# A decoder of two layers on one core: the self attentions with 16 heads take their values as weights, in column groups

## The chip, the cores and the metric

The kernel runs on one core of one Trainium2 chip. The metric is the time of one execution on the device in microseconds. All stages run in one program, one after the other, each with its own order of work for the five engines.

## The reference, cut to what matters

Input `x` is 8 sequences of 112 tokens with 512 features. Six blocks follow one another: self attention, cross attention, a second self attention with a routed MLP (layer 0), then self attention with low-rank updates, a joint attention and a routed MLP (layer 1). The change touches the first and the fourth block:

```python
def _L0_attn_ref(x, Wq, Wk, Wv, Wo):          # HEADS = 16, Dh = 32, T = 112
    q = (x @ Wq).reshape(B, T, H, Dh)         # k, v alike
    scores = jnp.einsum('bthd,bshd->bhts', q, k)
    scores = scores * jnp.tril(jnp.ones((T, T)))
    attn = jax.nn.softmax(scores / T ** 0.5, axis=-1)
    out = jnp.einsum('bhts,bshd->bthd', attn, v).reshape(B, T, H * Dh)
    return out @ Wo
def _L1_attn_ref(x, Wq, bq, Bq, Aq, ...):     # HEADS = 16, HEAD_DIM = 32
    q = _split(lora_linear(x, Wq, bq, Bq, Aq))    # k, v alike
    attn = jax.nn.softmax(jnp.einsum('bhqd,bhkd->bhqk', q, k) * SCALE, axis=-1)
    out = jnp.einsum('bhqk,bhkd->bhqd', attn, v)  # transposed and reshaped to [B, L, 512]
    return lora_linear(out, Wo, bo, Bo, Ao)
x = x + _L0_attn_ref(_layernorm(x), ...)
x = x + _L1_attn_ref(_layernorm(x), ...)
```

The mask of the first is a product, not an addition of minus infinity. The second has no mask.

## The kernel before

Each stage is a `Segment`, made of parts. A part has a small program for each engine and yields at fixed places. The segment plays the parts against each other by a list of letters: each letter lets its part go on to its next yield, on every engine. Engines go in order; between them stand only semaphores. `self_attention_order` (L2969) writes the list for the two segments of the change, `self0` (L3407) and `self3` (L3480s). In both, `p` is `QkvPart` (the projections, which also split each weight into a high and a low part, the low part on GpSimd at L1353), `a` is `SelfAttentionPart` (L1466) and `o` is `OutNormPart` (L2037, the output projection and the norm).

The list first runs half of the projections, then one `a` and one `p` in turn; when the projections are used up, one `a` and one `o` in turn; what is left of `o` comes last.

`SelfAttentionPart`: an item is four heads of one sequence, in one tile of 112x448. A step takes two items and has two yields, so two `a` of the list; a sequence has four items and two steps, so there are 16 steps and two more to drain. In the first half of step s, TensorE transposes the probabilities of the items of step s-2 (L1578) and makes the scores of step s (L1589, two items in alternation, each in its own 32 rows of the array). VectorE multiplies by the mask (L1618, `self0` only) and takes maxima (L1622), GpSimd subtracts them (L1565; in `self3` VectorE does, L1625), ScalarE copies the transposed probabilities of step s-2 out of PSUM (L1652). In the second half ScalarE takes the exponentials of step s (L1656), TensorE multiplies the transposed probabilities, as weights, with the values (L1602, 128 columns, of which column 32 is a column of ones and so gives the sum), and VectorE takes the reciprocal of the sum (L1632) and evacuates four heads times it (L1640).

`OutNormPart`: for each sequence, TensorE transposes the attention's output (L2278), ScalarE and VectorE split it into high and low (L2127, L2179), TensorE multiplies with Wo (12 products, L2246 to L2250), VectorE adds to `x` and takes moments (L2190 on), GpSimd the power for the norm (L2118), VectorE normalises (L2215, or L2217 with rounding to L2222 in `self0`), and TensorE transposes the normed rows (L2260) for `hT_hi` (ScalarE, L2130) and `hT_lo` (VectorE, L2167). A sequence enters every fourth `o`. So each pair of `a` and `o` has four kinds: after the first half of odd steps stands the split of the output, after the first half of even steps the 12 products, the rounding and `hT`, and after the second halves normalisation (odd) or addition and moments (even).

What the part does with an attention depends on `attention.turned`; a part with `turned = True` is one whose output lies in PSUM with features on the partitions.

## Time and profile before

| | us |
|---|---|
| median of 3 runs | 2788.76 (2788.07 to 2790.92) |
| the profiled execution, own time | 2790.01 |
| its span, first to last instruction | 2788.1 |
| TensorE busy in the span | 2570.0 (92%) |
| VectorE busy | 1694.7 (61%) |
| ScalarE busy | 1132.2 (41%) |
| GpSimd busy | 896.6 (32%) |
| mean granted TensorE clock | 0.955 of full |
| steps with scores in the first attention | 202.7 to 300.4 |
| the same in the second attention | 1595.7 to 1702.5 |

Busy shares are means over stages with different limits. A row of the timeline gives start, length, engine, line, operation, output and inputs, the count, and in brackets how long the engine stood idle before it and who released it. Rows of an engine overlap a little where it pipelines, so the distance of two starts says more than the length. A float32 product stands as two records on TensorE, so eight products are "x16"; the float32 transposes of two items are eight instructions, and 8 of their records stand in the row.

### The profile page before, as it was taken

Reading aid. Unit: us, or ns where it says so; the run is one execution under the profiler, and the core shown is the slowest. Engines: PE = TensorE matmul, PEld = TensorE weight load, DVE = VectorE, ACT = ScalarE, POOL = GpSimd, SP = SyncE. Lnnn points to the kernel's source line nnn. Section 1 sums busy time; section 2 is a strip of 40 time slices with the busy share of each in tenths; the row PEclk is TensorE's granted clock in tenths of the full one; section 3 lists DMA queues with packets and bytes.
Section 4 is the critical chain, followed back from the end, with each engine's and each line's share of the span. In section 5 each row is a group of like instructions: output and inputs, shape, how many; then the busy total and the mean of one; then the engine's idle time right before and its main releaser. Section 6 shows DMA issues by size and latency. Waiting matters only on the chain. (4 is left out here: it accounts for less than half of the span.)

```text
span 2788.1 us, 48182 instructions
## 1 busy us (share of the span) xinstructions
PE 2570.0 (92%) x14667; PEld 2065.4 (74%) x14668; DVE 1694.7 (61%) x3341; ACT 1132.2 (41%) x2434; POOL 896.6 (32%) x919
## 2 busy tenths in 40 slices
PE   8999799979899989799997898998999999899998
PEld 7888677768688877678875777774665678788887
DVE  4537757769776657567675566864434325666664
ACT  2113255533343324445453133755555522444443
POOL 3213100014332225423223200753333322345555
PEclk9999999999899979899998898999999989999999
DMA  5553122125532045388774432444222031566664
GB/s 188 154 144 99 31 92 63 59 66 154 162 104 64 15 142 172 123 235 224 193 213 120 112 73 70 131 132 149 73 64 73 22 128 55 154 163 161 162 153 81
DMA packets 289277, 332.87 MB, mean 119 GB/s; under 512 B 147445, under 2 KB 202693, under 8 KB 287312
## 3 DMA queue, kind: packets, MB, share of 16 engines
q1 hardware_dynamic: 217904, 252.57, 29.1%
q0 software_dynamic: 20640, 51.74, 9.6%
q10 hardware_dynamic: 50560, 26.34, 3.3%
q8 instruction: 99, 1.62, 0.2%
q14 instruction: 74, 0.61, 0.1%
HBM read 233.86 MB, written 96.72 MB: 119 GB/s over the span
## 5 line engine op out<-in xcount | busy, mean ns | idle before, releaser
L898 PE MATMUL e_psum<-e_up_hi,hT_hi 128*128 x672 | 245.2, 365 | 21.5 <-DVE hT_lo L867 14.6
L900 PE MATMUL e_psum<-e_up_hi,hT_lo 128*128 x672 | 236.7, 352 | 0.0
L899 PE MATMUL e_psum<-e_up_lo,hT_hi 128*128 x672 | 236.4, 352 | 0.0
L1920 POOL TENSOR_TENSOR joint_a_p<-joint_a_p,joint_a_rinv 112x487 f32<-112x487 f32 x128 | 125.2, 999 | 195.9 <-DVE joint_a_rinv L1966 195.5
L1565 POOL TENSOR_TENSOR self_a_p<-self_a_p,self_a_mx 112x448 f32<-112x448 f32 x96 | 96.0, 1000 | 205.2 <-DVE self_a_mx L1622 205.2
L898 PEld LDWEIGHTS e_psum<-e_up_hi,hT_hi 128*128 128x128 f32 x672 | 127.5, 190 | 43.6 <-issue 32.3
L1971 DVE TENSOR_REDUCE joint_a_mx<-joint_psum 112x1 f32<-112x487 f32 x128 | 85.0, 664 | 121.5 <-PE joint_psum L1941 121.2
L794 ACT ACTIVATE e_gate<-e_psum 128x352 f32<-128x352 f32 (+1 forms) x86 | 44.4, 516 | 256.4 <-PE e_psum L900 252.1
L873 DVE TENSOR_TENSOR hT_lo<-e_psum,hT_hi 128x256 fp32r<-128x256 f32 (+2 forms) x138 | 55.7, 435 | 142.1 <-ACT hT_hi L812 139.0
L1656 ACT ACTIVATE self_a_p<-self_a_p 112x448 f32<-112x448 f32 x128 | 71.6, 575 | 164.8 <-POOL self_a_p L1565 113.8
L900 PEld LDWEIGHTS e_psum<-e_up_hi,hT_lo 128*128 128x128 f32 x672 | 127.5, 190 | 11.5
L899 PEld LDWEIGHTS e_psum<-e_up_lo,hT_hi 128*128 128x128 f32 x672 | 127.7, 190 | 9.7
L1209 POOL TENSOR_TENSOR p_p_z<-p_p_straight,p_p_crossed 128x512 f32<-128x512 f32 x70 | 98.4, 1406 | 112.1 <-DVE p_p_crossed L1191 112.1
L828 DVE TENSOR_TENSOR e_up_lo<-e_up_raw,e_up_hi 128x1024 f32 (+3 forms) x128 | 128.0, 1051 | 3.2 <-issue 3.0
L766 POOL DMA_INDIRECT out<-e_y,e_back x51 | 123.2, 2416 | 17.3 <-issue 17.3
L847 DVE SCALAR_TENSOR_TENSOR e_act_raw<-e_gate,e_rows,e_psum 128x352 f32<-128x352 f32 (+1 forms) x86 | 55.4, 645 | 118.3 <-ACT e_gate L794 115.9
L898 PE MATMUL e_psum<-e_dn_hi,hT_hi 128*128 (+1 forms) x285 | 121.3, 426 | 1.0 <-issue 0.3
L1941 PE MATMUL joint_psum<-x_first,x_q 128*112 128x487 f32 x256 | 117.8, 582 | 1.8 <-PEq L89 1.7
L752 POOL TENSOR_TENSOR e_held<-e_zeros 1x1 f32<-1x1 f32 x90 | 19.7, 218 | 308.2 <-DVE e_idx L862 308.2
L142 PE MATMUL p_psum<-p_p_w_hi,hT_hi 128*128 128x512 f32 x280 | 115.5, 412 | 1.9 <-DVE p_p_w_lo L1175 1.9
L1994 ACT ACTIVATE joint_a_p<-joint_psum,joint_a_neg 112x487 f32<-112x487 f32 x128 | 85.4, 667 | 75.8 <-DVE joint_a_neg L1973 72.5
L781 ACT ACTIVATE e_up_hi<-e_up_raw 128x1024 f32 (+3 forms) x128 | 107.8, 923 | 15.1 <-PEq L89 15.1
(561 smaller groups left out, 7484.6 us busy)
## 6 DMA issues: line engine op xcount, KB each, us to landing
e_up_raw<-in_L_ffn_w SPq DMA_DIRECT2D x64, 512.0 KB, 4.8
e_up_raw<-in_L_ffn_w SPq DMA_DIRECT2D x64, 352.0 KB
e_dn_raw<-in_L_ffn_w SPq DMA_DIRECT2D x16, 1024.0 KB, 14.2
q_all<-p_p_t_stage ACTq DMA_DIRECT2D x56, 256.0 KB
e_dn_raw<-in_L_ffn_w SPq DMA_DIRECT2D x16, 512.0 KB
x_q<-q_all SPq DMA_DIRECT2D x8, 896.0 KB
v_ctx<-front_c_v_stage SPq DMA_DIRECT2D x24, 250.0 KB
x_others<-k_ctx SPq DMA_DIRECT2D x8, 750.0 KB, 4.6
```

Source lines behind the costliest of these rows:

```text
L142: last = pe.matmul(out, a, b, start=(k == 0 and i == 0), stop=(k == n_k - 1 and i == len(pairs) - 1))
L766: pool.indirect_dma_start(out=acc, out_offset=bass.IndirectOffsetOnAxis(ap=back[:, v, :], axis=0), in_=y[:, v, :], in_offset=None, compute ...
L781: act.activation(up_hi[:, bass.ds(slot * KC + k, 1), :], up_raw[:, k:k + 1, :], ACT.Copy).then_inc(up_hi_ready, 1)
L828: dve.tensor_tensor(up_lo[:, bass.ds(slot * KC + k, 1), :], up_raw[:, k:k + 1, :], up_hi[:, bass.ds(slot * KC + k, 1), :].bitcast(F32), AL ...
L898: pe.matmul(out, lhs[0], rhs[0], start=k == 0, stop=False)
L899: pe.matmul(out, lhs[0], rhs[1], start=False, stop=False)
L900: return pe.matmul(out, lhs[1], rhs[0], start=False, stop=k == n_k - 1)
L1209: both = pool.tensor_tensor(z[:, r, :], straight[:, r, :], crossed[:, r, :], ALU.add)
L1565: pool.tensor_tensor(p[:, i % RING, :, :], p[:, i % RING, :, :], mx[:, i % RING, :].unsqueeze(2).to_broadcast([T, group, T]), ALU.subtract ...
L1920: pool.tensor_tensor(p[:, r, :], p[:, r, :], rinv[:, r:r + 1].to_broadcast([T, S]), ALU.mult).then_inc(p_ready, 1)
L1941: pe.matmul(ps[0:T, s_banks[i % N_S], 0:S], q[:, b % 2, h, :], k[:, b % 2, h // group, :], start=True, stop=True).then_inc(s_done, 1)
L1994: act.activation(p[:, r, :], ps[0:T, s_banks[i % N_S], 0:S], ACT.Exp, bias=neg[:, r, :], scale=scale, accum_out=rsum[:, r:r + 1]).then_inc ...
```

## The change

`HeadSelfAttentionPart` takes the place of `SelfAttentionPart` in `self0` and `self3`. It has the same items, steps and lags, and is played by the same list. What differs:

- Values are the weights (112x32 of one head) and the transposed probabilities the moving operand. Four heads go to four column groups of the array, 32 columns each, and so to four groups of PSUM partitions: the output of a sequence lies with features on the partitions, 128x448. All 16 products of a sequence are made at once, in the second half of every second step.
- There is no column of ones. VectorE sums the exponentials of step s-1 in the second half of step s and takes one reciprocal for both items. GpSimd multiplies the exponentials by it. TensorE's transposes (lag 2 as before) wait for that product instead of for the exponentials.
- `OutNormPart` reads the output from PSUM (`turned`): its transposes of the output and its wait for VectorE's evacuation are gone, and so is the evacuation itself.
- The transposed probabilities have a ring of six instead of two.

```diff
+class HeadSelfAttentionPart:
...
+        dh, group, W, n_items, n_steps = 32, 4, 2, 4, 2
+        RING, PT, LT, LE = 6, 6, 2, 2
+        self.n_items, self.steps, self.lead, self.turned = 2 * n_steps, 2 + 2 * (B * n_steps + LE), 2 * LE, True
+        q = g.sb(f"{name}_q", [128, 2, 4, T])
+        k = g.sb(f"{name}_k", [128, 2, 4, T])
+        v = g.sb(f"{name}_v", [T, 2, D])
+        p = g.sb(f"{name}_p", [T, RING, group, T])
+        pt = g.sb(f"{name}_pt", [T, PT, group, T])
...
+        self.ot_done, self.o_used = pv_done, None
...
+        def rows_of(i):
+            r = i % n_items
+            return slice(r * dh, (r + 1) * dh)
...
+        def ot_view(i):
+            return ps[:, o_banks[i % N_O], 0:group * T].rearrange("p (c t) -> p c t", c=group)
+        self.ot_view = ot_view
...
+        def gpsimd(pool):
+            yield
+            yield
+            for step in range(n_all + LE):
+                for i in pair(step) if mask else []:
+                    pool.wait_ge(mx_ready, i + 1)
+                    pool.tensor_tensor(p[:, i % RING, :, :], p[:, i % RING, :, :], mx[:, i % RING, :].unsqueeze(2).to_broadcast([T, group, T]),
+                                       ALU.subtract).then_inc(less_ready, 1)
+                yield
+                for i in pair(step, 1):
+                    pool.wait_ge(rinv_ready, i // W + 1)
+                    pool.tensor_tensor(p[:, i % RING, :, :], p[:, i % RING, :, :], rinv[:, i % RING, :].unsqueeze(2).to_broadcast([T, group, T]),
+                                       ALU.mult).then_inc(p_ready, 1)
+                yield
+
+        def tensor(pe):
+            yield
+            yield
+            for step in range(n_all + LE):
+                for i in pair(step, LT):
+                    pe.wait_ge(p_ready, i + 1)
+                    reuse(pe, pt_ready, i - N_T + 1)
+                    for j in range(group):
+                        last = pe.transpose(ps[0:T, t_banks[i % N_T], j * T:(j + 1) * T], p[:, i % RING, j, :], core.ident[0:T, 0:T])
+                    last.then_inc(t_done, 1)
+                both = pair(step)
+                if both:
+                    b = step // n_steps
+                    if step % n_steps == 0:
+                        pe.wait_ge(qk_in[b % 2], 32 * (b // 2 + 1))
+                    reuse(pe, mask_done if mask else less_ready, both[-1] - N_S + 1)
+                    for j in range(group):
+                        for i in both:
+                            last = pe.matmul(ps[0:T, s_banks[i % N_S], j * T:(j + 1) * T], q[rows_of(i), b % 2, j, :],
+                                             k[rows_of(i), b % 2, j, :], start=True, stop=True)
+                            if j == group - 1:
+                                last.then_inc(s_done, 1)
+                yield
+                at = step - LT
+                if at >= 0 and at % n_steps == n_steps - 1:
+                    b = at // n_steps
+                    pe.wait_ge(v_in[b % 2], 16 * (b // 2 + 1))
+                    pe.wait_ge(pt_ready, (b + 1) * n_items)
+                    reuse(pe, self.o_used, b - N_O + 1)
+                    for j in range(group):
+                        for i in range(b * n_items, (b + 1) * n_items):
+                            h = j * group + i % n_items
+                            last = pe.matmul(ps[rows_of(i), o_banks[b % N_O], j * T:(j + 1) * T], v[:, b % 2, h * dh:(h + 1) * dh],
+                                             pt[:, i % PT, j, :], start=True, stop=True)
+                    last.then_inc(pv_done, 1)
+                yield
...
+            for step in range(n_all + LE):
+                for i in pair(step):
...
+                yield
+                before = pair(step, 1)
+                for i in before:
+                    dve.wait_ge(exp_done, i + 1)
+                    dve.tensor_reduce(rsum[:, i % RING, :], p[:, i % RING, :, :], AX.X, ALU.add).then_inc(sum_ready, 1)
+                if before:
+                    at = before[0] % RING
+                    dve.wait_ge(sum_ready, before[-1] + 1)
+                    dve.reciprocal(rinv[:, at:at + W, :], rsum[:, at:at + W, :]).then_inc(rinv_ready, 1)
+                yield
...
+                for i in pair(step, LT):
+                    act.wait_ge(t_done, i + 1)
+                    reuse(act, pv_done, (i - PT) // n_items + 1)
...
@@ head_qkv, self0, self3 @@
-            return 32, p, lambda b: q32[b], lambda b: k32[b], lambda b: v_self[b, 0, 0:T, :], 16
+            return p, lambda b: q32[b], lambda b: k32[b], lambda b: v_self[b, 0, 0:T, :]
-                    a = SelfAttentionPart(g, "a", *head_qkv(p), float(T) ** -0.5, (2, 3), (4, 5), (6, 7), "tril", ALU.mult)
+                    a = HeadSelfAttentionPart(g, "a", *head_qkv(p), float(T) ** -0.5, (2, 3), (4, 5), (6, 7), "tril")
-                a = SelfAttentionPart(g, "a", *head_qkv(p), 32.0 ** -0.5, (2, 3), (4, 5), (6, 7))
+                a = HeadSelfAttentionPart(g, "a", *head_qkv(p), 32.0 ** -0.5, (2, 3), (4, 5), (6, 7))
```

On TensorE, in the steady part of the first attention, before: transposes of one item, the scores of the next step, then the output part's transposes.

```order
L1578 MATMUL self_psum<-ident,self_a_p 112x112 [waits self0_a_pt_ready,self0_a_exp_done]
L1578 MATMUL self_psum<-ident,self_a_p 112x112 x3
L1589 MATMUL self_psum<-self_a_k,self_a_q 112x112 [waits self0_a_mask_done]
L1589 MATMUL self_psum<-self_a_k,self_a_q 112x112 x7
L2278 MATMUL self_psum<-ident,self_a_o 128x112 [waits self0_o_lo_ready,self0_a_o_evac]
L2278 MATMUL self_psum<-ident,self_a_o 128x112 x3
```

Now:

```order
L1750 MATMUL self_psum<-ident,self_a_p 112x112 [waits self0_a_pt_ready,self0_a_p_ready]
L1750 MATMUL self_psum<-ident,self_a_p 112x112 x3
L1760 MATMUL self_psum<-self_a_k,self_a_q 112x112 [waits self0_a_mask_done]
L1760 MATMUL self_psum<-self_a_k,self_a_q 112x112 x7
L1774 MATMUL self_psum<-self_a_pt,self_a_v 32x112 [waits self0_o_lo_ready,self0_a_pt_ready,self0_a_v_in0]
L1774 MATMUL self_psum<-self_a_pt,self_a_v 32x112 x15
L1750 MATMUL self_psum<-ident,self_a_p 112x112 [waits self0_a_pt_ready,self0_a_p_ready]
```

The transposes wait for `p_ready` (GpSimd's product) instead of `exp_done`; the scores still stand behind them. Of the output part's transposes nothing is left, and the 16 value products are one group.

On VectorE, at the end of the first half of a step and through its second half, before:

```order
L1618 TENSOR_TENSOR self_a_p<-self_psum,self_a_mask 112x448 [waits self0_a_t_done,self0_a_s_done]
L1622 TENSOR_REDUCE self_a_mx<-self_a_p 112x4 [waits self0_a_mask_done]
L1402 COPY self_p_stage<-self_psum 112x512 [waits self0_p_stored3,self0_p_mm_done]
L2179 TENSOR_TENSOR self_o_oT_lo<-self_psum,self_o_oT_hi 128x448 [waits self0_o_hi_ready]
L1632 RECIPROCAL self_a_rinv<-self_psum 112x4 [waits self0_a_pv_done]
L1640 TENSOR_TENSOR self_a_o<-self_psum,self_a_rinv 112x4x32 [waits self0_a_rinv_ready]
L1632 RECIPROCAL self_a_rinv<-self_psum 112x4 [waits self0_a_pv_done]
L1640 TENSOR_TENSOR self_a_o<-self_psum,self_a_rinv 112x4x32 [waits self0_a_rinv_ready]
```

Now (`L1790` is the mask, `L1794` the maxima, `L2345` the low part of the output):

```order
L1790 TENSOR_TENSOR self_a_p<-self_psum,self_a_mask 112x448 [waits self0_a_t_done,self0_a_s_done]
L1794 TENSOR_REDUCE self_a_mx<-self_a_p 112x4 [waits self0_a_mask_done]
L1402 COPY self_p_stage<-self_psum 112x512 [waits self0_p_stored3,self0_p_mm_done]
L2345 TENSOR_TENSOR self_o_oT_lo<-self_psum,self_o_oT_hi 128x448 [waits self0_o_hi_ready]
L1803 TENSOR_REDUCE self_a_rsum<-self_a_p 112x4 [waits self0_a_exp_done] x2
L1807 RECIPROCAL self_a_rinv<-self_a_rsum 112x8 [waits self0_a_sum_ready]
L1790 TENSOR_TENSOR self_a_p<-self_psum,self_a_mask 112x448 [waits self0_a_t_done,self0_a_s_done]
```

Two evacuations with two reciprocals make place for two sums and one reciprocal, in the same position behind the mask and the maxima.

On GpSimd, from the start of `self0`, before:

```order
L2110 MEMSET self_o_expo 112x1
L1353 TENSOR_TENSOR x_others<-self_p_w_raw,x_others 128x512 [waits self0_p_hi_ready] x4
L1565 TENSOR_TENSOR self_a_p<-self_a_p,self_a_mx 112x448 [waits self0_a_mx_ready] x8
L1353 TENSOR_TENSOR x_first_lo<-self_p_w_raw,x_first_hi 128x512 [waits self0_p_hi_ready] x4
L1565 TENSOR_TENSOR self_a_p<-self_a_p,self_a_mx 112x448 [waits self0_a_mx_ready] x6
L2872 MEMSET x_others 128x6x96 [waits self0_p_mm_done]
L2118 TENSOR_TENSOR self_o_rstd<-self_o_var_eps,self_o_expo 112x1 [waits self0_o_var_ready,self0_o_expo_set]
```

Now (`L1733` subtracts the maxima, `L1738` multiplies by the reciprocals):

```order
L1353 TENSOR_TENSOR x_others<-self_p_w_raw,x_others 128x512 [waits self0_p_hi_ready] x4
L1733 TENSOR_TENSOR self_a_p<-self_a_p,self_a_mx 112x448 [waits self0_a_mx_ready] x4
L1738 TENSOR_TENSOR self_a_p<-self_a_p,self_a_rinv 112x448 [waits self0_a_rinv_ready] x2
L1733 TENSOR_TENSOR self_a_p<-self_a_p,self_a_mx 112x448 [waits self0_a_mx_ready] x2
L1738 TENSOR_TENSOR self_a_p<-self_a_p,self_a_rinv 112x448 [waits self0_a_rinv_ready] x2
L1733 TENSOR_TENSOR self_a_p<-self_a_p,self_a_mx 112x448 [waits self0_a_mx_ready] x2
L1353 TENSOR_TENSOR x_first_lo<-self_p_w_raw,x_first_hi 128x512 [waits self0_p_hi_ready] x4
L1738 TENSOR_TENSOR self_a_p<-self_a_p,self_a_rinv 112x448 [waits self0_a_rinv_ready] x2
L1733 TENSOR_TENSOR self_a_p<-self_a_p,self_a_mx 112x448 [waits self0_a_mx_ready] x2
```

The products stand between the subtractions, in pairs. Those of the third step's pair stand behind the split of Wo (`x_first_lo`, four instructions).

## Rows read from the trace of the kernel before

**Rows 1.** Windows, a steady stretch: busy us (instructions) of each engine, then PEclk, DMA share, GB/s.
```profile
260.00:280.00 20.00, 18.80 (x166) 16.48 (x164) 18.28 (x45) 7.54 (x15) 6.83 (x8) 0.91 0.29 66
```

**Rows 2.** Timeline, TensorE, score products and last value products, first attention: start, duration.
```profile
208.76 1.04 PE L1589 MATMUL self_psum<-self_a_k,self_a_q 32*112 32x112 f32 x16
245.24 1.04 PE L1589 MATMUL self_psum<-self_a_k,self_a_q 32*112 32x112 f32 x16
300.37 1.04 PE L1589 MATMUL self_psum<-self_a_k,self_a_q 32*112 32x112 f32 x16
313.90 1.97 PE L1602 MATMUL self_psum<-self_a_v,self_a_pt 112*112 112x128 f32 x16 [0.35 <-ACT self_a_pt L1652]
```

**Rows 3.** Timeline, TensorE, score products of the second attention.
```profile
1601.66 1.04 PE L1589 MATMUL self_psum<-self_a_k,self_a_q 32*112 32x112 f32 x16
1648.84 1.04 PE L1589 MATMUL self_psum<-self_a_k,self_a_q 32*112 32x112 f32 x16
1702.47 1.04 PE L1589 MATMUL self_psum<-self_a_k,self_a_q 32*112 32x112 f32 x16
```

**Rows 4.** Timeline, TensorE, one batch of the first attention.
```profile
276.02 1.04 PE L1589 MATMUL self_psum<-self_a_k,self_a_q 32*112 32x112 f32 x16
277.43 1.91 PE L1602 MATMUL self_psum<-self_a_v,self_a_pt 112*112 112x128 f32 x16
279.19 0.93 PE L1578 MATMUL self_psum<-ident,self_a_p 112*112 112x112 f32 x8
280.70 1.04 PE L1589 MATMUL self_psum<-self_a_k,self_a_q 32*112 32x112 f32 x16 [0.59 <-DVE self_a_p L1618]
284.67 0.55 PE L2260 MATMUL self_psum<-ident,self_p_w_raw 112*128 112x112 f32 x4
```

**Rows 5.** Timeline, VectorE, projection phase (first row) and the same batch.
```profile
212.47 0.62 DVE L1398 COPY self_p_stage<-self_psum 128x448 f32<-128x448 f32 x1 [0.17 <-PE self_psum L1453]
...
274.19 0.62 DVE L2167 TENSOR_TENSOR hT_lo<-self_psum,hT_hi 128x448 fp32r<-128x448 f32 x1 [0.76 <-ACT hT_hi L2130]
276.11 0.17 DVE L1632 RECIPROCAL self_a_rinv<-self_psum 112x4 f32<-112x4 f32 x1
278.75 0.62 DVE L1618 TENSOR_TENSOR self_a_p<-self_psum,self_a_mask 112x448 f32<-112x448 f32 x1
279.41 0.62 DVE L1622 TENSOR_REDUCE self_a_mx<-self_a_p 112x4 f32<-112x448 f32 x1
281.13 0.61 DVE L2179 TENSOR_TENSOR self_o_oT_lo<-self_psum,self_o_oT_hi 128x448 fp32r<-128x448 f32 x1
281.66 0.17 DVE L1632 RECIPROCAL self_a_rinv<-self_psum 112x4 f32<-112x4 f32 x1
282.49 0.54 DVE L2217 TENSOR_SCALAR self_p_w_raw<-x_tok,self_o_mv,self_o_rstd 112x512 f32<-112x512 f32 x1
```

**Rows 6.** Timeline, GpSimd and ScalarE, first attention.
```profile
226.22 5.01 POOL L1353 TENSOR_TENSOR x_first_lo<-self_p_w_raw,x_first_hi 128x512 fp32r<-128x512 f32 x4
231.19 1.83 POOL L1565 TENSOR_TENSOR self_a_p<-self_a_p,self_a_mx 112x448 f32<-112x448 f32 x2
...
273.61 0.54 ACT L2130 ACTIVATE hT_hi<-self_psum 128x448 fp32r<-128x448 f32 x1 [3.13 <-PE self_psum L2260]
```

**Rows 7.** Timeline, TensorE, an idle stretch, the window behind it, and scores at the lower clock.
```profile
267.50 1.04 PE L1589 MATMUL self_psum<-self_a_k,self_a_q 32*112 32x112 f32 x16 [1.14 <-DVE self_a_p L1618]
...
268.60:272.00 3.40, 3.40 (x8) 2.47 (x9) 3.16 (x10) 1.43 (x3) 0.42 (x1) 0.52 0.43 114
...
752.84 1.84 PE L1589 MATMUL self_psum<-x_first_hi,x_wp_hi 64*112 64x112 f32 x16 [0.23 <-DVE self_a_p L1618]
```

**Rows 8.** One VectorE line (min/median/max ns), its slow one, and GpSimd beside it.
```profile
L2221 DVE TENSOR_SCALAR self_p_w_raw<-self_p_w_raw x8: 426/427/1039, 261.5 to 339.2; 112x512 f32<-112x512 f32 x8
261.50 1.04 DVE L2221 TENSOR_SCALAR self_p_w_raw<-self_p_w_raw 112x512 f32<-112x512 f32 x1
261.14 1.10 POOL L1565 TENSOR_TENSOR self_a_p<-self_a_p,self_a_mx 112x448 f32<-112x448 f32 x1 [0.25 <-DVE self_a_mx L1622]
```

69 lines of the change are left out of this document (added).

## The prediction

> **What bounds the kernel now.** I read in this order: the busy time by stage, the spacing of the score products on TensorE, then each engine through one batch.
>
> In a step of an attention two items (four heads each) pass. TensorE transposes the probabilities of two steps ago (T), makes this step's scores (S) and lies one step ahead. VectorE masks and takes maxima (phase A1), then evacuates values (phase A2). One phase of the output part stands after each; "even" and "odd" steps differ in which. In the steady stretch VectorE is busy 18.28 of 20 us and TensorE 18.80 [rows 1]: both are near full, and neither waits long. S waits only for the mask of the step before (idle 0.59 us) [rows 4]. The ten steps of the first attention that carry no projections take 300.37 - 245.24 = 55.13 us for nine intervals [rows 2]; in the second 1702.47 - 1648.84 = 53.63 [rows 3]. The five intervals before them take 36.48 and 47.18 us; projections fill TensorE there.
>
> **The change, engine by engine.** VectorE loses two evacuations per step, 282.49 - 281.66 = 0.83 us [rows 5]. It gains two row sums of 112x448; the nearest row is the maximum of the same shape, 0.62 us, and four such operations of A1 go at 281.13 - 278.75 = 2.38, so two cost 1.19. One reciprocal with its gap adds 0.22 (0.17 and 0.05). That is +0.58 us per step.
>
> TensorE loses four transposes of the output per batch, 277.43 - 276.02 - 1.04 = 0.37 us, and its 16 value products, 2 x (279.19 - 277.43) = 3.52 us, become 16 of 32 output rows [rows 4]. The trace has no column groups. The nearest row is S, which alternates two row groups: 8 products in 1.04 us, 0.13 each; a value product takes 0.22. So 16 cost 2.1 us, with bounds 0.9 (four abreast) and 3.5 (no overlap). I take 2.1; it doesn't enter the sum, as TensorE gets idle time.
>
> GpSimd gains 32 multiplications per attention. The subtraction of the same shape is the nearest row: two in 1.83 us [rows 6].
>
> The price is in a wait. T of step s-1 used to wait for exponentials, long ready. It now waits for the multiplication, which waits for the reciprocal, which stands in A2 of step s behind A1 of step s. And S of step s+1 stands behind that T on TensorE, while A1 of step s+1 waits for S. So every step becomes one closed loop: S, A1, output phase, sums, reciprocal, multiplication, T, S. What VectorE does after the reciprocal (1.4 to 1.8 us of output work) lies beside it and hides nothing of it.
>
> Loop without output work: S 1.04 [rows 4], hop 0.03, A1 2.38, sums 1.19, reciprocal 0.22 [rows 5], hop 0.05, two multiplications 1.83 [rows 6], hop 0.05, second half of T 0.43 (0.93 for eight records, rows 4). Sum 7.22 us. From A2 to the next S it is 3.77.
>
> - Odd steps add oT_lo, 281.66 - 281.13 = 0.53 [rows 5]: 7.75.
> - Even steps of the first attention: step 6 adds nothing (7.22); step 8 adds the rounding, 276.11 - 274.19 - 0.53 = 1.39 (8.61). From step 10 hT_lo waits for ScalarE, which waits for transposes behind the 12 output products: 284.67 - 280.70 = 3.97 after S begins [rows 4], 0.58 for the transposes, 0.57 for ScalarE (0.54 long, rows 6), hT_lo 0.53, rounding 1.39, then 3.77: 10.81.
> - In the second attention there is no rounding: 7.22 for steps 6 and 8, 9.42 from step 10.
>
> First: 7.22 + 8.61 + 3 x 10.81 + 4 x 7.75 = 79.3, against 55.1: +24.1. Second: 2 x 7.22 + 3 x 9.42 + 4 x 7.75 = 73.7 against 53.6: +20.1.
>
> Steps 1 to 5, first attention. A projection's evacuation comes between A1 and A2: it starts 212.47 - 208.76 = 3.71 after S, lasts 0.54, then 3.77: 8.0 us. Steps 1 and 2 take that. In step 3 the multiplications stand behind Wo's split, 5.01 us [rows 6], and that behind this step's subtractions: A1 ends 3.45 after S, subtraction 0.98, split 5.01, multiplication 1.83, T 0.48: 11.75. Steps 4 and 5 with the wider value groups about 8.4 and 8.9. Sum 45.1 against 36.5: +8.6. Second attention: its five steps already take 9.4 us on the mean, more than the 8.0 to 8.9 of the loop, so only its shorter steps can grow, and no subtraction stands before the split. I estimate +3.5, between 0 and the first one's 8.6. Bounds of both together: 0 (hidden under projections) and 17.
>
> Tail: from S of step 15 to the last value products 313.90 - 300.37 = 13.5 us now. Then: 7.75, output products and transposes 2.93 + 0.58, ScalarE to rounding 2.49, 3.77, one copy 0.5: 18.0, less 0.4 for the output's transposes: +4.1. The same 4 for the second. Bounds 0 and 6 each.
>
> Sum at full clock: 24.1 + 20.1 + 8.6 + 3.5 + 8.1 = 64.4 us.
>
> **Clock.** TensorE would work some 8 to 9 us of the 15 to 18.6 of a batch, in bursts with 3 to 5 us of idle between. TensorE had idled 1.14 us before 267.50, and the granted clock was 0.52, the 1.2 GHz level, from 268.6 to 272.0 [rows 7]; so it will fall often. At that level S takes 1.84 us [rows 7] against 1.04, +0.8 on the loop, and the half T of 0.43 about +0.4 if it doubles: 21.6 us for 18 steps. Eight of twelve output products took 3.40 us there against 2.0 at the other level's 0.25 (3.0 over 12, rows 4): +1.4 to 1.6 in six steps, 9.6. All low costs 31, none 0. I take half, 15.
>
> 64.4 + 15 = 79.4. The profiled execution took 2790.0 us (span 2788.1 and 1.9 around it), so 2869.4; the median of before lies 1.2 lower: **2868 us**.
>
> **Port.** A scaling of 112x512 on VectorE took 1.04 us instead of 0.43 with a subtraction of 1.10 instead of 0.93 beside it on GpSimd [rows 8]: the two engines can hold each other up. The multiplication starts 0.05 after the reciprocal, just when h (0.54) starts on VectorE in the odd steps. I take nothing for it and keep up to 8 us for the range (0.5 in five odd steps of the first, 1.1 in the second, which adds a bias too).
>
> The Trainium skill, "SBUF — State Buffer", section "SBUF: two separate sides", says that the pair of ports shared by VectorE and GpSimd is locked for a whole instruction, by VectorE operations in a two-port mode or with two SBUF inputs, against a GpSimd operation that reads SBUF. The slow row agrees. By it the 8 us would fall due, and the time would be 2876.
>
> **Rivals.**
>
> 1. *VectorE's queue alone decides.* Normalisation hides behind output work, and the time grows by 0.58 x 36 steps at most: 21 us, likelier 10, as the early steps have slack: 2800. For it: VectorE is the fuller of the engines late in a batch. Against: the order of waits leaves no room. Chance 0.06.
> 2. *The loop closes only in the steady steps*, at full clock; projections and tail hide the rest: 44.2 us, 2833. Chance 0.12.
> 3. *The clock stays low and the port costs its 8*: 64 + 31 + 8 = 103, 2892. Chance 0.13.
> 4. *Faster: TensorE bounds and the wait is hidden.* Its stream has 18.80 of 20 us busy. Each batch frees 3.52 - 2.1 + 0.37 = 1.8 us, 29 for 16 batches: 2760. It decides if the multiplications end before TensorE comes to T, that is if TensorE has some 3.5 us of other work between S and T more than VectorE has. Only steps with two projection groups come near. Chance 0.04. The Trainium skill, "TensorEngine Tiling (Array Packing)", section "Theoretical Speedup", gives up to 4x for a dimension of 32; with it the value products would cost 0.9 us and this case would end at 2741. The trace shows 0.13 against 0.22 us for two groups, and no four.
> 5. *The change does nothing that can be measured*: sums, products and waits balance. Chance 0.03.
>
> **Numbers.** The forecast has 0.62: loop closed throughout, clock between the levels, 2850 to 2885. With rivals 2 and 3 the range is 2828 to 2893; 0.13 lies below with rivals 1, 4, 5, the rest is error of the terms. A measurement of this kernel tells about 0.2% from none. Slower by more than that: 0.62 + 0.12 + 0.13 + 0.06 = 0.93; same 0.03; faster 0.04.
>
> **What would show it.** In the profile after, T's first product waits for the multiplication in nearly every step, VectorE's mask waits for S some 1.5 to 2 us per step, and VectorE's busy share in both attentions falls although it has more work. S to S is near 7.7 in odd and 9.5 to 11 in even steps. In the projection phase of the first attention one interval is near 12 us, behind Wo's split. The granted clock is well under 1.00 there. Outside both attentions nothing moves. If T waits for nothing, or S to S stays near 6 us, the central step is wrong; if intervals are right at full clock, only the clock term is.

## The result, and the profile after

The changed kernel takes **2910.9 us** (2908.0 to 2914.65, 4 runs) against 2788.64 of the kernel before in the same job: ratio 1.0436, 95% interval 1.0423 to 1.0449. The forecast was 2868 with a range of 2828 to 2893: the direction and the mechanism hold, the size does not. The profiled execution has a span of 2912.9 us against 2788.1 and a mean granted clock of 0.923 against 0.955. These two spans differ by 124.8 us, the medians by 122.3, so 2.5 us of what follows is the spread of single executions.

The steady steps of both attentions first, as windows of the kernel after (columns as in [rows 1]), from the scores of step 6 to those of step 15:
```profile
258.12:353.97 95.85, 62.26 (x417) 46.69 (x416) 56.48 (x118) 22.69 (x43) 37.22 (x42) 0.62 0.16 46
1723.19:1813.98 90.79, 58.74 (x417) 43.60 (x417) 54.68 (x102) 24.86 (x47) 22.40 (x23) 0.67 0.14 38
```
They answer to the 55.13 and 53.63 us of [rows 2, 3]. There TensorE and VectorE were both near full. Now TensorE is busy 62 of 96 us and VectorE 56: no engine is full, and the clock is 0.62. That is the look of a closed loop.

Timeline of the kernel after, first attention, the loop of one odd step (start, length, and in brackets idle and releaser):
```profile
284.93 1.77 PE L1760 MATMUL self_psum<-self_a_k,self_a_q 32*112 32x112 f32 x16
286.63 1.72 PE L1774 MATMUL self_psum<-self_a_pt,self_a_v 112*32 112x112 f32 x32
286.72 0.62 DVE L1790 TENSOR_TENSOR self_a_p<-self_psum,self_a_mask 112x448 f32<-112x448 f32 x1 [2.59 <-PE self_psum L1760]
289.11 0.61 DVE L2345 TENSOR_TENSOR self_o_oT_lo<-self_psum,self_o_oT_hi 128x448 fp32r<-128x448 f32 x1
289.63 1.14 DVE L1803 TENSOR_REDUCE self_a_rsum<-self_a_p 112x4 f32<-112x448 f32 x2
290.81 0.20 DVE L1807 RECIPROCAL self_a_rinv<-self_a_rsum 112x8 f32<-112x8 f32 x1
291.09 2.02 POOL L1738 TENSOR_TENSOR self_a_p<-self_a_p,self_a_rinv 112x448 f32<-112x448 f32 x2 [0.89 <-DVE self_a_rinv L1807]
292.27 1.89 PE L1750 MATMUL self_psum<-ident,self_a_p 112*112 112x112 f32 x8 [3.92 <-POOL self_a_p L1738]
294.09 1.84 PE L1760 MATMUL self_psum<-self_a_k,self_a_q 32*112 32x112 f32 x16
296.01 0.62 DVE L1790 TENSOR_TENSOR self_a_p<-self_psum,self_a_mask 112x448 f32<-112x448 f32 x1 [3.48 <-PE self_psum L1760]
300.02 0.55 PE L2426 MATMUL self_psum<-ident,self_p_w_raw 112*128 112x112 f32 x4
```
Read it as a ring: scores to mask 1.79 us (1.07 predicted), phase A1 2.39 (2.38), oT_lo 0.52 (0.53), sums 1.18 (1.19), reciprocal 0.28 (0.27), products and last transposes 3.00 (2.31). Sum 9.16 against 7.75. Every VectorE step is right to 0.02 us; both excesses are TensorE at its lower level (scores 1.77 to 1.84 where [rows 4] had 1.04; eight transposes 1.89 for 0.93), but for 0.2 on GpSimd, whose pair takes 2.02 with VectorE's h beside it. In the even step behind it, the transposes that follow the output products start 300.02 - 294.09 = 5.93 us after the scores, where [rows 4] had 3.97.

The wait itself, over both attentions (one line of the kernel after, the transposes, and what its engine idled for):
```profile
L1750 PE MATMUL self_psum<-ident,self_a_p x256: 258/392/438, 214.8 to 1833.9; 112*112 112x112 f32 x128
its engine sat idle before it (us, times) until:
  POOL self_a_p L1738: 102.6, 46
```

Where the 124.8 us of span went, by starts of the score products and of the next stage (the tail is the time from the scores of step 15 to the next stage):

| part | predicted | measured |
|---|---|---|
| steps 6 to 14, first / second | 24.1 / 20.1 | 40.7 / 37.2 |
| steps 1 to 5, first / second | 8.6 / 3.5 | 13.5 / 4.9 |
| tail, first / second | 4.1 / 4.0 | 7.1 / 10.9 |
| clock, all parts | 15 | in the rows above |
| outside both attentions | 0 | 10.6 (not due to the change, see below) |
| start of the first scores, both together | 0 | 0.0 |

The rows for step 1 and the tail (answering to [rows 2]), and those of steps 3 to 5:
```profile
208.12 1.04 PE L1760 MATMUL self_psum<-self_a_k,self_a_q 32*112 32x112 f32 x16
...
224.72 1.84 PE L1760 MATMUL self_psum<-self_a_k,self_a_q 32*112 32x112 f32 x16
237.38 1.84 PE L1760 MATMUL self_psum<-self_a_k,self_a_q 32*112 32x112 f32 x16
248.93 1.04 PE L1760 MATMUL self_psum<-self_a_k,self_a_q 32*112 32x112 f32 x16
258.12 1.84 PE L1760 MATMUL self_psum<-self_a_k,self_a_q 32*112 32x112 f32 x16
...
353.97 1.84 PE L1760 MATMUL self_psum<-self_a_k,self_a_q 32*112 32x112 f32 x16
375.79 1.72 PE L1774 MATMUL self_psum<-self_a_pt,self_a_v 112*32 112x112 f32 x32 [0.67 <-issue]
```
Step 3 takes 12.66 us (11.75 predicted, behind Wo's split). Step 4 takes 11.55 where 8.4 was predicted; VectorE's next row says why, beside TensorE's products of the same time:
```profile
244.27 0.63 PE L1453 MATMUL self_psum<-x_others,hT_hi 128*112 128x512 f32 x2
244.47 0.69 DVE L1402 COPY self_p_stage<-self_psum 112x512 f32<-112x512 f32 x1 [2.76 <-PE self_psum L1453]
```
The projection's evacuation, ahead of the row sums, starts 244.47 - 237.38 = 7.09 us after the scores instead of 3.71 [rows 2, 5]. TensorE is not idle in between: it makes the scores in 1.84 us and then twelve products of the projection, 0.43 us each from start to start at its lower level and 0.23 where the clock is up again (244.27 on).

### The profile page after: what moved, and what is told of

It is laid out like the page before. It is cut to its first block and busy times, and to the rows that moved or that the text cites. A ratio compares the mean times of both kernels' runs of the same rounds, so it can differ in the third digit from the quotient of the medians.

```text
span 2912.9 us, 48005 instructions
## 1 busy us (share of the span) xinstructions
PE 2592.0 (89%) x14603; PEld 2057.0 (71%) x14604; DVE 1712.4 (59%) x3309; ACT 1134.8 (39%) x2434; POOL 955.9 (33%) x981
## 5 line engine op out<-in xcount | busy, mean ns | idle before, releaser
L2137 DVE TENSOR_REDUCE joint_a_mx<-joint_psum 112x1 f32<-112x487 f32 x128 | 85.0, 664 | 122.6 <-PE joint_psum L2107 122.3
L1750 PE MATMUL self_psum<-ident,self_a_p 112*112 112x112 f32 x256 | 51.5, 348 | 102.8 <-POOL self_a_p L1738 102.6
L1738 POOL TENSOR_TENSOR self_a_p<-self_a_p,self_a_rinv 112x448 f32<-112x448 f32 x64 | 63.2, 1008 | 182.7 <-DVE self_a_rinv L1807 182.7
L1750 PEld LDWEIGHTS self_psum<-ident,self_a_p 112*112 112x112 f32 x256 | 33.7, 173 | 121.5 <-POOL self_a_p L1738 121.4
L766 POOL DMA_INDIRECT out<-e_y,e_back x51 | 113.8, 2231 | 16.7 <-issue 16.7
```

The lines of the kernel that those rows point to most:

```text
L766: pool.indirect_dma_start(out=acc, out_offset=bass.IndirectOffsetOnAxis(ap=back[:, v, :], axis=0), in_=y[:, v, :], in_offset=None, compute ...
L1750: last = pe.transpose(ps[0:T, t_banks[i % N_T], j * T:(j + 1) * T], p[:, i % RING, j, :], core.ident[0:T, 0:T])
L2137: dve.tensor_reduce(mx[:, r, :], ps[0:T, s_banks[i % N_S], 0:S], AX.X, ALU.max).then_inc(mx_ready, 1)
```

## Experiments

Theory L: the closed loop through the wait is the cause. Rival W: the added operations themselves are. Theory C: a large part of the loop's length is TensorE's clock, which is low in a loop that leaves TensorE idle. Ratios are to the kernel before in the same job, with the 95% interval in square brackets. "Stages" are the first and second attention against before, which has 0 and 0; the changed kernel has +60.7 and +53.6.

**Scores first.** TensorE makes a step's scores before the transposes that wait.
```
             for step in range(n_all + LE):
-                for i in pair(step, LT): ... transposes
                 both = pair(step)          # scores
                 ...
+                for i in pair(step, LT): ... transposes
```


> In each step TensorE makes the scores of step s before the transposes of step s-2; nothing else is changed. Theory L (the closed loop of scores, masks, sums, product, transposes): scores no longer stand behind the product, so the loop opens; VectorE's queue decides, 0.58 us per step more than before. In the profile scores to scores go back to about 6.5 to 7 us, the granted clock in both attentions is above 0.95, and the time is 2805 us (2790 to 2820). Rival W (the added work itself, the shared port and the changed value products cost the time, wherever the scores stand): the time stays within 15 us of 2911.

2850.95 us, 1.0227 [1.0208, 1.0247]: stages +21.8 and +29.8. Half of the loss is gone by order alone, less than L expected (2805, bounds 2790 to 2820). The trace has another loop in its place, over two steps: steps 12 and 13 of the first attention take 17.4 us together, where the changed kernel takes 23.1 and the kernel before 12.7. Timeline of this kernel, TensorE and VectorE:
```profile
295.44 1.04 PE L1754 MATMUL self_psum<-self_a_k,self_a_q 32*112 32x112 f32 x16
296.12 0.62 DVE L2333 TENSOR_TENSOR hT_lo<-self_psum,hT_hi 128x448 fp32r<-128x448 f32 x1 [4.06 <-ACT hT_hi L2296]
298.04 1.14 DVE L1803 TENSOR_REDUCE self_a_rsum<-self_a_p 112x4 f32<-112x448 f32 x2
300.49 1.89 PE L1762 MATMUL self_psum<-ident,self_a_p 112*112 112x112 f32 x8 [4.00 <-POOL self_a_p L1738]
```
The scores wait no more, but the output products and their turn stand behind the waiting transposes; VectorE waits 4.06 us for their result, and the row sums stand behind that.

**Product left out, and done twice.** The first leaves the normalisation out (its output is not normalised); the second lets GpSimd make each product once more, into a spare tile.
```
-  for i in pair(step, 1): pool.tensor_tensor(p.., rinv.., mult).then_inc(p_ready, 1)
-  pe.wait_ge(p_ready, i + 1)
+  pe.wait_ge(exp_done, i + 1)
```


> GpSimd's multiplication is left out (the output is not normalised) and the transposes wait for the exponentials; the sums and reciprocals stay, and so do the new value products. Theory L: as with scores first, about 2800 us (2785 to 2815), a little less since GpSimd holds no port. Rival W in the form that sums or value products cost the time: above 2850. The distance to scores first tells what the product costs by its work alone: under 10 us.

> Each multiplication on GpSimd is made twice, the first into a tile that nobody reads. Theory L: every step's loop gets 2 x 0.93 us longer, in 16 to 17 steps of each attention: 33 x 1.86 = +61 us against 2911, so 2972 (2960 to 2985). A theory in which the product is mostly hidden and low clock comes from elsewhere gives under +15.

Left out (two executions): 2818.4 us, 1.0102, stages +2.6 and -0.2, although row sums and reciprocals are still there. What it takes over before is not in the attentions: the stretch with the experts between them took 34.8 us more, and its weight loads of the first product count 288 instead of 264. I take it that other values route tokens otherwise; no run tests that. Twice (two executions): 2996.42, 1.074: +85.5 us for 32 x 1.86 = 60 us of work, above L's bounds (2960 to 2985). In the steady steps the loop charges the price and a hand-over: an odd step of the first attention takes 11.3 us for 9.24. Most of the rest is in steps 1 to 5, which grow by 35 us in both attentions for 19 of work; from step 3 on their scores now take 1.84 us, and the mean granted clock of the whole is 0.906. Both speak for L, against W.

**Product on VectorE.** The same product behind the reciprocal, on VectorE (1.16 us the pair).
```
                     dve.reciprocal(...).then_inc(rinv_ready, 1)
+                    dve.wait_ge(rinv_ready, before[0] // W + 1)
+                for i in before:
+                    dve.tensor_tensor(p.., p.., rinv.., ALU.mult).then_inc(p_ready, 1)
```


> The product of probabilities and reciprocals stands on VectorE, right behind the reciprocal, instead of GpSimd. Theory L: the loop has 2 x 0.62 = 1.24 us in place of 1.83 and two hops of 0.05, so each of 36 steps is 0.69 us shorter, 25 us in all, 2886 us, though VectorE has 40 us more to do. Rival W (VectorE's work is what costs): 1.24 x 32 = 40 us more, 2950.

2883.85 us, 1.033 [1.0314, 1.0346]: 27 less than the change (29 less if each is taken against before in its own job), 25 expected, with some 37 us (32 x 1.16) more for VectorE to do. The shorter ring wins over the fuller engine: W falls.

**Three steps late.** The transposes take the probabilities of three steps ago, so that the product is a step old.
```
-        RING, PT, LT, LE = 6, 6, 2, 2
+        RING, PT, LT, LE = 6, 6, 3, 3
```


> The transposes take the probabilities of three steps ago instead of two; three value groups of buffers more, one more step of drain in each attention, no operation added or left out. Theory L (closed loop: TensorE's transposes wait for a product made in the same step): the product that they need is now a step old, nothing waits for it, the scores start as soon as the mask is done. Both attention stages return to before plus VectorE's 0.58 us a step where VectorE is full, plus one more step of drain (5 to 8 us each): 2788 + 8 + 13 = about 2809 us, bounds 2795 to 2825. The granted clock in the steady steps rises with it. Rival W (the added work itself costs, wherever it stands): within 15 us of 2911.

2799.13 us, 1.0028 [1.0017, 1.004]; stages -1.4 and +8.0. One step more of distance takes back 114 of 122 us with every added operation in place (8 are left against before in the same job), as L expected (2809, bounds 2795 to 2825). It does not make the change a gain. The transposes' line in this kernel:
```profile
L1750 PE MATMUL self_psum<-ident,self_a_p x256: 257/259/437, 218.7 to 1724.0; 112*112 112x112 f32 x128
its engine sat idle before it (us, times) until:
  POOL self_a_p L1738: 15.0, 13
```
15.0 us of waiting instead of 102.6, and a median of 259 ns instead of 392. The granted clock over the steady steps is 0.78 and 0.74, above the 0.62 and 0.67 of the changed kernel, but well below the 0.97 that both attentions had before: with the wait went part of the lower clock, not most of it.

**Filled idle time**, twice: products that nothing reads, between a step's scores and the next transposes; 24 from step 6, then 20 in the first attention from step 3 and 14 in the second from step 6.
```
+                if both and step >= 6:
+                    pe.wait_ge(pt_ready, W * (step - LT) + W)
+                    for _ in range(24): pe.matmul(<64 spare columns>, ident, ident[.., 0:64])
```


> From step 6 on, TensorE makes 24 small products without use in the second half of each step (112x64 of the identity, into a free part of a transposes' bank), about 2.6 us at the full clock, in the time in which it waits for GpSimd. Theory C (low clock is what the forecast mis-sized: some 25 us in each attention over the sum at full clock): granted clock above 0.95 in the steady steps, odd steps near 7.9 and even ones near 11 us, and the time falls by 25 to 40 us, to 2871 to 2886. Rival P (the shared port and longer hand-overs are the missing time, and the low clock is idle time that costs nothing): the time stays within 8 us of 2911 or rises.

> Adds idle-time products (20 in the first attention from step 3, 14 in the second from step 6) on TensorE between a step's scores and the next transposes, into a part of a bank that nothing reads; fewer than the 24 tried before, so that they end before the product that the transposes wait for. Theory C (of the 124 us, a large part is TensorE's clock at its lower level, because the loop leaves it idle): granted clock 0.9 or more from step 6 on in both attentions, odd steps 8.0 and even ones 9.4 to 10.8 as in the first filled run, now in both attentions: 25 to 40 us less than 2911, so 2871 to 2886. Rival P (the loop's length is set by VectorE and GpSimd alone, TensorE's pace doesn't matter): within 8 us of 2894, the first filled run, or above it.

24 (two executions): 2894.25, 1.0374; 14 and 20: 2921.6, 1.046 [1.0441, 1.048], 11 us worse than no filling. As totals both miss C's numbers, and the second is on its rival's side. The 24 take 4.8 us at the full clock, not the 2.6 expected. The filling delays the loop itself while the clock is low (20 products took 4.06 us before the score products of step 13 and 7.73 before the next; step 6 with 24 took 11.9 us for 8.2), and in the second run it did not hold the clock. What they do settle is the loop at full clock. Windows of the first filled kernel, steps 7 to 14 of both attentions:
```profile
271.63:345.54 73.91, 70.96 (x765) 63.40 (x765) 51.11 (x107) 20.54 (x40) 32.50 (x36) 1.00 0.12 33
1722.18:1797.58 75.40, 71.70 (x766) 64.38 (x765) 49.11 (x91) 22.35 (x44) 19.95 (x20) 0.98 0.17 46
```
The same steps of the changed kernel:
```profile
266.35:353.97 87.62, 54.33 (x381) 40.88 (x380) 51.60 (x110) 20.48 (x39) 33.05 (x37) 0.63 0.11 32
1731.31:1813.98 82.67, 51.03 (x381) 38.05 (x381) 49.63 (x93) 22.65 (x43) 20.58 (x21) 0.67 0.15 41
```
Transposes and scores of the first filled kernel around one odd step:
```profile
307.87 1.04 PE L1760 MATMUL self_psum<-self_a_k,self_a_q 32*112 32x112 f32 x16
314.51 0.58 PE L1750 MATMUL self_psum<-ident,self_a_p 112*112 112x112 f32 x4
315.39 0.59 PE L1750 MATMUL self_psum<-ident,self_a_p 112*112 112x112 f32 x4 [0.30 <-POOL self_a_p L1738]
315.91 1.04 PE L1760 MATMUL self_psum<-self_a_k,self_a_q 32*112 32x112 f32 x16
```
In the first attention, at clock 1.00, an odd step takes 8.04 us (7.75 predicted) and each even one from step 10 takes 10.79 (10.81 predicted); in the changed kernel they take 9.2 from step 9 on and 13.3 to 14.2. Steps 7 to 14 take 73.9 us here and 87.6 there: 13.7 us are clock. In the second attention they take 75.4 and 82.7: at least 7.3 us are clock, for here the filling itself outlasts GpSimd's product in some even steps (in step 8 the product ends at 1737.40 and the transposes start at 1739.19). The first attention's tail is 60.1 us at clock 0.72 in the changed kernel and 56.1 at 0.88 here: another 4.0.

**Sums on TensorE.** Can the feature-major form pay? Ones as weights give the sums in column groups, VectorE divides per sequence behind the value products; no row sums, no product on the ring.
```
+  for j, i: pe.matmul(ps[rows_of(i), o_banks[1], ..], ones[:, :], pt[:, i % PT, j, :])
+  dve.reciprocal(o[:, :, :], total); dve.tensor_tensor(o[:, :, :], out, o[:, :, :], ALU.mult)
```


> The value products keep their column groups and the output its feature-major form, but nothing is normalised before the transposes: sixteen more products of a 112x32 block of ones per sequence give the sums, already spread over the 32 rows of each head, and VectorE takes one reciprocal of 128x448 and one product of 128x448 per sequence behind the value products. Row sums, their reciprocals and GpSimd's products are gone. Theory L: the wait is gone from the loop, TensorE has 16 x 0.12 = 1.0 to 1.9 us more per sequence than in the changed kernel and still 2 less than before the change, VectorE has per sequence two large operations (0.62 each if the reciprocal runs like the mask, up to 3 in all if it doesn't) against four evacuations of 0.42 before. So 2780 us, bounds 2765 to 2805. Rival: the feature-major form and the column groups are themselves slow, whatever the normalisation does: over 2850.

2797.61 us, 1.0022 [1.0013, 1.0031]. The rival (over 2850) falls; the expected 2780 (bounds 2765 to 2805) does not come. VectorE is busy 14.15 of the 14.81 us of a batch, and this row is the part of it that was taken for less:
```profile
280.82 2.96 DVE L1809 RECIPROCAL self_a_o<-self_psum 128x448 f32<-128x448 f32 x1
```
A reciprocal of 448 columns takes 2.96 us, where a product of the shape takes 0.62.

**Sums by the exponentials**, on top of three steps late: ScalarE's accumulated output in place of VectorE's row sums, for both items of a step, for one, and for both with five filling products.
```
+  for j in range(group):
+      last = act.activation(p[.., j, :], p[.., j, :], ACT.Exp, scale=scale, accum_out=rsum[.., j:j + 1])
```


> On top of the transposes three steps late: the row sums are taken by ScalarE as the accumulated output of four exponentials of 112x112 per item, in place of one of 112x448, and VectorE's two row sums per step (1.14 us) are gone. Theory V (with the wait gone, what stands above the kernel before is VectorE's 1.14 us a step; it is 12.7 of 14.2 us busy in a batch): VectorE 10.4 us a batch, ScalarE 4.85 + 4 x 1.4 = 10.5 (0.20 for each read of an accumulator, from the rows of the other attentions), TensorE some 9 to 10: a batch of 11.5 to 12.5 us, 1.5 to 2.5 less in some 12 batches: 2799 - 24 = 2775 us, bounds 2760 to 2795. Rival A (ScalarE's four short instructions delay the evacuation of the transposed probabilities, which stands behind them on its queue, and TensorE waits for it): 2799 or more, up to 2830.

> The same for one of the two items of a step, the other's row sum stays on VectorE: VectorE 11.6 us a batch, ScalarE 7.7. Theory V: half of the gain, 2787 us (2775 to 2797). Rival A: ScalarE's delay is half as long and is hidden by its idle time: then this one is faster than the run with both, at 2780 to 2790.

> On top of the version with transposes three steps late and sums by the exponentials: five idle-time products, 1.0 us at the full clock, between the scores of an odd step and the transposes of the next, where TensorE waits 1.0 us for GpSimd's product. Their result is read by nothing. A batch there takes 13.7 us, with the twelve output products at half clock for 4.7 us of it. Theory C (what is left above the loop's own length is the lower clock): the clock stays up through the output products, a batch falls to 12 to 12.5 us, about 10 batches in the two attentions gain 1.2 each: 2780 us, bounds 2770 to 2790. Rival P: the pause of 1.1 us before the scores of the even step is enough to let the clock fall, the filler then takes 2 us at half clock and lengthens the batch: 2795 to 2810.

Both items 2792.01, 0.9993 [0.9983, 1.0002]; one item 2797.65, 1.0023 [1.0014, 1.0032]; filled 2790.83, 1.0001 [0.9989, 1.0013]. The first and the third can't be told from before, the second is 0.1 to 0.3% slower: no version is faster than the kernel before. With both items 7 to 8 of the 24 us that theory V expected come, at the upper end of its bounds (2760 to 2795), and one item brings next to nothing (2797.65, just above V's 2775 to 2797): VectorE was not the last bound. The filled one lies between the bounds of C (to 2790) and of P (from 2795). A batch of the run with both items still takes 13.7 us (14.3 without the new sums), with VectorE busy 10.65:
```profile
273.82:287.51 13.69, 11.29 (x97) 8.66 (x97) 10.65 (x24) 7.31 (x38) 8.03 (x10) 0.75 0.19 52
```
In the filled kernel, one batch (steps 11 and 12 of the first attention) takes 277.11 - 266.22 = 10.89 us at clock 1.00, and the next, at 0.75, takes 13.5. By this one batch, what is left is TensorE at its lower level; how to hold it up stays open.

## Why the prediction was wrong

**Right.** The wait of the transposes, in nearly every step; the ring's order; VectorE's terms. With the changed kernel's own 8.23 us for step 6 and the filled run's 73.9 for steps 7 to 14, the loop itself costs at most 82.1 - 55.1 = +27.0 in the first attention, where the sum had 24.1. Step 3 behind the split was 0.9 short. The value products cost 0.06 us each at the full clock (32 records in 0.97), not the 0.13 that I took; the term was kept out of the sum, and rightly, as TensorE idles. The Trainium skill, "TensorEngine Tiling (Array Packing)", section "Theoretical Speedup", gives up to 4x for a dimension of 32. The trace agrees, with 3.6 times (3.52 to 0.97 us for 16 products), and the kernel still is slower: that is the lesson of the case.

**The step that failed** is the clock: "All low costs 31, none 0. I take half, 15." The lower level cost at least 28 us: 13.7 and 7.3 in steps 7 to 14 of the two attentions, 4.0 in the first tail, and 3.1 in step 4 of the first attention (0.8 on the scores and 2.3 on the twelve projection products ahead of the evacuation). Three things were wrong in the term. The level is not halfway: over the steady steps the granted clock is 0.62 and 0.67, where 0.5 is the 1.2 GHz level throughout and 0.75 the half that I took, and the scores take 1.66 to 1.84 us in 17 of the 20 steps from 6 to 15. The term covered only the steady steps; steps 1 to 5 and the tails were priced at full clock. And "all low" was itself too small: its +1.4 to 1.6 us for the output products is what eight of the twelve cost (3.40 for 2.0). In step 14 of the first attention the twelve take 5.1 us (341.50 to 346.64), 2.1 more than 3.0.

The clock is the largest term, but not all. The sum of 79.4 was 45.4 us short; at least 13 of these are the clock's excess over 15, 10.6 lie outside both attentions, and most of the rest is in the second attention.

**In the second attention the loop itself was priced too low.** At clock 0.98 steps 7 to 14 take 75.4 us, where the sum had 66.5 for them (four of 7.75, 7.22 for step 8, three of 9.42). Some of the 8.9 is the filling's own delay, but odd steps, where the transposes wait for GpSimd and not for the filling, take 8.49 us and once 9.10 instead of 7.75. The port, put at nothing, is most of this: GpSimd's pair takes 2.48 us for 1.82, beside VectorE's bias row of 1.42, which takes 0.68 where GpSimd is idle (in the first attention's odd steps the pair takes 2.02):
```profile
1775.89 2.48 POOL L1738 TENSOR_TENSOR self_a_p<-self_a_p,self_a_rinv 112x448 f32<-112x448 f32 x2 [6.73 <-DVE self_a_rinv L1807]
1776.15 1.42 DVE L2329 TENSOR_TENSOR x_tok<-x_tok,self_o_b_row 112x512 f32<-112x512 f32 x1
1786.76 0.68 DVE L2982 TENSOR_TENSOR x_first<-self_f_raw,x_first 128x512 fp32r<-128x512 f32 x1
```
Over five odd steps each, the port costs 1.0 and 3.3 us, within the 8 kept for it. The bias row has two inputs in SBUF and GpSimd's product reads SBUF, the case in which the Trainium skill, "SBUF — State Buffer", section "SBUF: two separate sides", has one lock the other out; the trace agrees. The last row is a step that I had missed: the split of the next stage's weights stands ahead of the row sums in steps 12 and 13, 0.6 us on the ring each time (1787.35 - 1786.76).

The second tail was set to "the same 4" as the first. But in the kernel before it is shorter: from the scores of step 15 to the last value products 1713.28 - 1702.47 = 10.8 us, against 13.5 in the first [rows 2]. After the change it is 20.9. In the first filled kernel, whose clock is up until the last of its waits, it is 17.9: I estimate the clock's part of the +10.1 at 3 to 4 us.

**Outside.** "Outside both attentions nothing moves" failed by 10.6 us, in stages whose instructions did not change. 4.9 of them are in the cross attention (254.5 us against 249.6), most of it in one stretch, from 150 to 175 us behind its start, where the granted clock was 0.79 against 0.86. They can't be put down to the loop. The cross attention takes 254.7 us with the product left out, where the loop is gone, and 249.9 to 250.2 in both filled kernels and with the product on VectorE, where it is there. From its end to the second attention 918.6 us became 922.0, and four other kernels have 918.3 to 922.9. What decides it is open.

Rival 3 (clock low throughout, port due: 2892) named the right mechanism, and was short too, since it priced the clock in the steady steps alone and had the same short loop for the second attention. The others fall: rival 1, VectorE's queue alone, with the product on VectorE, which gave VectorE more to do and was faster; rival 2, loop closed in the steady steps only, with the +18.4 us of steps 1 to 5 and the +18.0 of the tails; rivals 4 and 5, faster or no change, with the ratio.

## What to carry to other kernels

When an edit puts an engine's result between two phases of the same step, walk the ring once around before counting work: its length per step, not any engine's busy time, is the new time. The cure is a step more of distance, two constants here. And if a ring leaves TensorE idle for several us per step, price all its work in every stage behind the wait at the lower clock; a half was no cautious middle here. A second use of the same part needs its own sum: its neighbours on VectorE and its tail are other ones.

## What the runs showed of the hardware

- Sixteen value products over four column groups, weights of 112x32 and 112 moving columns in float32: 0.97 us for 32 records at the full clock, 1.72 at the lower one, where 16 products with 128 output columns took 3.52 [rows 4].
- VectorE's reciprocal of 128x448 float32 from PSUM: 2.96 us, 4.8 times a product of the shape; one of 112x8: 0.20.
- Four exponentials of 112x112, each with its accumulated sum read out, take 1.18 us from start to start of the next item's (274.19 to 275.37 in the kernel with both items); one of 112x448 takes 0.58. The 1.4 us that I expected as extra cost of an item was more than twice too high.
- GpSimd's pair of products of 112x448 takes 1.82 us alone and 2.48 beside a VectorE addition of 112x512 with both inputs in SBUF, and that addition 1.42 instead of 0.68.
- Filling TensorE's pauses is fragile: 24 products held the scores at 1.04 us from step 7 to the end of the first attention, 20 lost that level behind step 11.
